# Moving the scaling multiply of two quantised feed-forward stages from VectorE to GpSimd, with the units five ahead

## The reference, cut to what matters

```
def fp4_quant_dequant(x):                 # blocks of 16 along the last dim
    scale = max(max(abs(xb)) / 6.0, 1e-12)
    xn = xb / scale
    idx = searchsorted(_MID, abs(xn))     # grid 0, .5, 1, 1.5, 2, 3, 4, 6
    return _GRID[idx] * sign(xn) * scale

gate = fp4_linear(x, w_gate)              # 128 -> 352
y    = fp4_linear(x, w_up)                # 128 -> 352
h    = silu(gate) * y
return fp4_linear(h, w_down)              # 352 -> 128

x = x + 0.5 * _L1_ffn_ref(_layernorm(x), ...)     # stages four and six
```

## Time and profile before

| | us |
|---|---|
| median of 3 runs (2184.43 to 2184.46) | 2184.46 |
| the profiled execution, its own time | 2185.35 |
| its span in the profile | 2183.3 |
| PE busy (share of the span) | 1894.8 (87%) |
| DVE busy | 1719.8 (79%) |
| ACT busy | 1094.0 (50%) |
| POOL busy | 737.7 (34%) |

### The profile page before, as it was taken

The page is one execution under the profiler, slowest core; times in us unless marked ns, Lnnn a source line. Parts: engine busy times, 40 slices in busy tenths (PEclk is TensorE's granted clock), DMA queues, the critical chain, the costliest instruction groups (busy, mean ns, idle before and its releaser), DMA issues.

```text
span 2183.3 us, 66263 instructions
## 1 busy us (share of the span) xinstructions
PE 1894.8 (87%) x27657; PEld 1452.5 (67%) x27657; DVE 1719.8 (79%) x3976; ACT 1094.0 (50%) x2876; POOL 737.7 (34%) x835
## 2 busy tenths in 40 slices
PE   0999899998999677768999999999999999767775
PEld 0888566665888455546777777777777777645553
DVE  5566688888566799976888888888888888579995
ACT  0444333332444445445666666666666666344542
POOL 1000577775000122213444444444444444212221
PEclk9999999999999799988999999999999999879997
DMA  4000000000000000000000000000000000000002
GB/s 110 1 1 2 1 2 2 2 2 1 1 1 1 1 0 1 1 1 2 3 3 3 3 3 3 3 3 3 3 3 3 3 3 3 3 1 1 1 1 77
DMA packets 14551, 14.42 MB, mean 7 GB/s; under 512 B 1392, under 2 KB 12080, under 8 KB 14256
## 3 DMA queue, kind: packets, MB, share of 16 engines
q1 hardware_dynamic: 14256, 10.20, 1.7%
HBM read 6.01 MB, written 4.19 MB: 5 GB/s over the span
## 4 chain that ended last, share of the span: by engine, by line
PE 64%; DVE 22%; POOL 5%; ACT 4%; issue 4%; SPq 0%; DVEq 0%; POOLq 0%; DMA 0%
PE acc L472 6%; PE acc L449 5%; PE acc L1652 5%; PE acc L1642 4%; POOL arena L933 4%; PE acc L749 4%; PE acc L1664 3%; DVE arena L897 3%; DVE arena L890 3%; PE acc L767 3%; DVE arena L900 3%; ACT arena L946 3%; PE acc L1694 2%; PE acc L463 2%; DVE arena L1209 2%
## 5 line engine op out<-in xcount | busy, mean ns | idle before, releaser
L1492 POOL TENSOR_TENSOR arena<-arena 128x288 f32<-128x288 f32 (+1 forms) x384 | 292.1, 767 | 460.3 <-ACT arena L1399 400.9
L933 POOL TENSOR_TENSOR arena<-arena 128x960 f32<-128x960 f32 (+2 forms) x70 | 118.0, 1685 | 576.1 <-DVE arena L900 576.1
L1399 ACT ACTIVATE arena<-acc 64x288 f32<-64x288 f32 x384 | 155.4, 405 | 143.9 <-PE acc L1670 136.4
L1218 DVE SCALAR_TENSOR_TENSOR arena<-acc,arena 128x288 f32<-128x288 f32 (+1 forms) x384 | 157.0, 409 | 71.0 <-PE acc L1664 39.9
L424 ACT ACTIVATE arena<-acc,wib 128x256 f32<-128x256 f32 x256 | 100.3, 475 | 151.2 <-PE acc L463 151.2
L1002 PE MATMUL acc<-wguT,arena 128*128 128x352 f32 x256 | 117.4, 544 | 60.5 <-DVE arena L872 57.0
L1024 PE MATMUL acc<-wdT,arena 128*128 128x128 f32 (+1 forms) x768 | 105.8, 289 | 69.9 <-ACT arena L961 69.0
L667 POOL TENSOR_TENSOR arena<-arena,quadcol 128x512 f32<-128x512 f32 x64 | 65.2, 1040 | 289.6 <-DVE arena L545 289.6
L1024 PEld LDWEIGHTS acc<-wdT,arena 128*128 128x128 f32 (+1 forms) x768 | 93.3, 196 | 85.5 <-ACT arena L961 85.5
L1664 PE MATMUL acc<-arena 64*64 64x72 f32 (+1 forms) x3072 | 135.3, 224 | 11.7 <-DVE arena L1218 11.7
L1652 PE MATMUL acc<-arena 64*64 64x72 f32 (+1 forms) x3072 | 134.0, 224 | 13.0 <-DVE arena L1209 12.6
(11 more groups left out here) (240 smaller groups left out, 4951.5 us busy)
## 6 DMA issues: line engine op xcount, KB each, us to landing
out_dram<-X SPq DMA_DIRECT2D x4, 1024.0 KB, 9.3
wi<-in_wiT_dram SPq DMA_DIRECT2D x1, 256.0 KB, 2.7
wout<-in_woT_dram SPq DMA_DIRECT2D x1, 256.0 KB, 3.3
wqkv<-in_w_qkv_dram SPq DMA_DIRECT2D x1, 192.0 KB, 2.7
arena<-in_w_down_dram SPq DMA_DIRECT2D x1, 176.0 KB, 2.5
arena<-in_w_gate_dram SPq DMA_DIRECT2D x1, 128.0 KB, 2.1
arena<-in_w_up_dram SPq DMA_DIRECT2D x1, 128.0 KB, 2.2
wq<-in_WqT_dram SPq DMA_DIRECT2D x1, 64.0 KB, 2.3
```

What stands on the lines that cost most here:

```text
L933: pool.tensor_tensor(b3(zq[s][:, cols]), b3(rnd[s][:, cols]), each(small[s][:, 1, blocks(n)]), ALU.mult).then_inc(zq_ready, 1)
L1218: dve.scalar_tensor_tensor(pm[s][:, group[g], cols], pn[s][:, group[g], cols], part, tm[s][:, group[g], cols], ALU.mult, ALU.add).then_inc ...
L1399: ins = act.mul(sq[s][rows, group[g], :], pn[s][other, group[g], 0:MW], part)
L1492: pool.tensor_tensor(tm[s][:, group[g], cols], pm[s][:, group[g], cols], sq[s][:, group[g], cols], ALU.subtract).then_inc(tm_ready, 1)
```

## The change

LEAD becomes 5, and the buffers z, y, big, rnd and zq become three deep (DEEP = 3, indexed by unit modulo 3). The pairs of small per-block arrays (scale and reciprocal) exist four times (`kept`), and two more arrays, the block maximum and the maximum with the margin (`top`), lie in PSUM bank 7 (`peak`). The turned x moves to the second half of bank 6, beside the output of `down`. The large multiply of `scale` is done by POOL (`scaled`), with the margin put into `top` by one more small instruction on DVE; y has now its true sign, so the first rounding instruction subtracts. All four programs get a new order, with scale and split of one unit three turns apart. In the last stage `finish` takes no statistics.

```
-            LEAD = 3
+            LEAD, DEEP = 5, 3
+            kept = LEAD - 1
+            last = phase == len(plan)
-            xT = psum[:, 7, 0:SEQ]
+            xT = psum[:, 6, SEQ:2 * SEQ]
+            peak = psum[:, 7, 0:2 * kept * NZ].rearrange("p (u c b) -> p u c b", u=kept, c=2)
...
                 def finish(n):
-                    for j in range(TPB):
+                    if not last:
                         dve.wait_ge(added, n + 1)
-                        dve.wait_ge(masks, 1)
-                        dve.bn_stats(...)
+                        for j in range(TPB):
+                            dve.bn_stats(...)
...
+                def scale(u):
+                    if u >= LEAD:
+                        dve.wait_ge(hid_ready, u - LEAD + 1)
+                    if u < NB:
+                        dve.wait_ge(xn_ready, u + 1)
+                    amax, top = (peak[:, u % kept, c, blocks(u)] for c in range(2))
+                    scl, inv = (small[u % kept][:, c, blocks(u)] for c in range(2))
+                    dve.tensor_reduce(amax, b3(z[u % DEEP][:, part(u)]), AX, ALU.max, apply_absolute_value=True)\
+                       .then_inc(amax_ready, 1)
+                    dve.wait_ge(amax_ready, u + 1)
+                    c = chain.did(dve.tensor_scalar(top, amax, (1.0 + 2.0 ** -22) / 6.0, 1e-12, ALU.mult, ALU.max))
+                    dve.tensor_scalar(scl, amax, 1.0 / 6.0, 1e-12, ALU.mult, ALU.max).then_inc(scl_ready, 1)
+                    chain.settle(c)
+                    dve.reciprocal(inv, top).then_inc(inv_ready, 1)
...
-                for n in range(NB):          # hidden, scale(n+3), finish(n-2), split(n+3)
+                for n in range(-LEAD, NB + 5):
+                    if 0 <= n + 2 < NB + LEAD:
+                        split(n + 2)
+                    if 0 <= n < NB:
+                        hidden(n)
+                    if 0 <= n - 5:
+                        finish(n - 5)
+                    if n < NB:
+                        scale(n + LEAD)

             def g(pool):
+                def scaled(u):
+                    k = u % DEEP
+                    pool.wait_ge(inv_ready, u + 1)
+                    pool.tensor_tensor(b3(y[k][:, part(u)]), b3(z[k][:, part(u)]), each(small[u % kept][:, 1, blocks(u)]),
+                                       ALU.mult).then_inc(y_ready, 1)
+                def restore(u):              # waits hT_done, xT_done, rnd_ready(u), scl_ready(u)
+                    ...
+                for n in range(-4, NB + 3):
+                    if 0 <= n + 2:
+                        restore(n + 2)
+                    if 0 <= n + 4 < NB + LEAD:
+                        scaled(n + 4)
...
+            ACT, n from -6: gated(n+1) twice, turned_x(n+2), magnitude(n+4), turned(n-3), norm(n+6);
+                norm(n) waits y_ready(n-3)
+            PE, n from -2: gates(n+1), turn_x(n+2), turn_hidden(n-3), down(n-4);
+                turn_x(n) waits xqT_ready(n-1) and added(n-6); turn_hidden(n) waits hqT_ready(n-1);
+                down(n) waits xqT_ready(n+6) and added(n-1)
```

More of the change, by code:

```diff
@@ L818, in fp4_ffn @@
             HX, HH = TPB * D, TPB * FH
-            LEAD = 3
+            LEAD, DEEP = 5, 3
+            U = range(DEEP)
+            kept = LEAD - 1
+            last = phase == len(plan)
             HZ = HX + HH
             NZ, NX = HZ // BLK, HX // BLK
[L823 to L827, removed]
+            z = [cut(HZ) for _ in U]
+            y = [cut(HZ) for _ in U]
+            big = [cut(HZ) for _ in U]
+            rnd = [cut(HZ) for _ in U]
+            zq = [cut(HZ) for _ in U]
             xqT = [cut(SEQ) for _ in R]
@@ L870, in hidden @@
+                def hidden(n):
                     dve.wait_ge(sig_ready, (n + 1) * TPB)
                     dve.wait_ge(up_done, (n + 1) * TPB)
[L872 to L898, removed]
-                    chain.settle(k)
-                    dve.scalar_tensor_tensor(rnd[s][:, cols], big[s][:, cols], FLOOR, rnd[s][:, cols],
+                    dve.tensor_tensor(hid[(n + LEAD) % DEEP], sig[n % STREAMS], ups, ALU.mult).then_inc(hid_ready, 1)
@@ L901, in split @@
+                def split(u):
+                    dve.wait_ge(big_ready, u + 1)
+                    k, cols = u % DEEP, part(u)
+                    c = chain.did(dve.scalar_tensor_tensor(rnd[k][:, cols], big[k][:, cols], FLOOR, y[k][:, cols],
+                                                           ALU.max, ALU.subtract))
+                    chain.settle(c)
+                    dve.scalar_tensor_tensor(rnd[k][:, cols], big[k][:, cols], FLOOR, rnd[k][:, cols],
                                              ALU.max, ALU.subtract).then_inc(rnd_ready, 1)
@@ L906, in v @@
                 dve.sem_inc(normed, 1)
-                scale(0, 0)
-                scale(1, 1)
-                split(0, 0)
-                scale(2, 0)
-                split(1, 1)
-                split(2, 0)
-                for n in range(NB):
-                    s = n % STREAMS
-                    hidden(n, s)
-                    scale(n + LEAD, 1 - s)
-                    if n >= STREAMS:
-                        finish(n - STREAMS)
-                    split(n + LEAD, 1 - s)
-                for s in R:
-                    finish(NB - STREAMS + s)
@@ L958, in turned @@
+                def turned(n):
+                    s = n % STREAMS
                     for j in range(TPB):
@@ L1029, in t @@
                 pe.wait_ge(*prepare.done)
[L1030 to L1044 removed]
+                for n in range(-2, NB + 4):
+                    if 0 <= n + 1 < NB:
+                        gates(n + 1)
+                    if n + 2 < NB:
+                        turn_x(n + 2)
+                    if 0 <= n - 3 < NB:
+                        turn_hidden(n - 3)
+                    if 0 <= n - 4 < NB:
+                        down(n - 4)
             vec.append(v), ten.append(t), sca.append(a), gps.append(g)
```

132 lines of the change are left out of this document (57 added, 75 removed).

## The result

The changed kernel takes 2109.94 us (median of 4 runs, 2103.83 to 2112.18) against 2184.46 (2184.43 to 2187.32) for the kernel before, measured beside it: a ratio of 0.9658, 95% interval 0.9645 to 0.967. The forecast was 2128 with a range from 2111 to 2154. The direction and the main mechanism were right. The gain was larger than any case allowed: 74.5 us against 56.4, and against 72.8 in the most hopeful one.

What follows compares the result with a forecast made beforehand. VectorE was taken to bound the kernel before in the two changed stages, at 7.39 us a turn. First stage -25.7 and last -30.7, together -56.4, took 2185.35 to 2129.0; the median, 0.9 lower, gave 2128, range 2111 to 2154.

Steps and rivals of the forecast that it cites:

- the most hopeful one: Whole kernel: the ends cost nothing more and the clock never drops; 72.8 us saved, 2112 us, chance 0.05.
- the port excludes, and it sets the turn: Quantised stages: VectorE's two roundings and GpSimd's multiplies exclude each other, a chain of 6.11 us, binding in the last stage.
- rival 1: GpSimd's multiplies are dearer beside VectorE, 0.25 us more each, a turn of 6.65 in both stages; 2150 us, chance 0.12.
- The wait for the magnitude: VectorE's hole before the first rounding, ended by ScalarE's magnitude, goes: -0.21 us a turn.
- +0.19: VectorE's turn: cost in us of one more small tensor_scalar, between 0.1 and 0.5.
- 6.30: First stage: VectorE's turn in us, from 7.39 - 1.07 - 0.21 + 0.19, longer than the chain with 0.1 to spare.
- 6.17: Last stage: turn in us set by the chain of two roundings and GpSimd's two multiplies, with a hand-over.
- the statistics left out in the last one: Last stage: VectorE's work falls by 0.49 us a turn, of which only 0.13 is had.
- +2.4 a stage: Both stages: three drops of TensorE's clock make `finish` late, +2.4 us a stage, between 0 and 5.
- the ends: Each stage: small units -4.5 us, filling +3.5, emptying +2.3; in the last, statistics of the last five pairs -1.5.
- Rival 3: GpSimd's scaling slips between the two roundings and holds VectorE 1.82 us more a turn; 2216 us, chance 0.06.
- A read costs nothing: VectorE reading PSUM: reciprocals of 128 columns take 948 ns from PSUM and 943 from SBUF.

Runs made afterwards that it cites:

- Experiments 2 to 4: Changed kernel with statistics in neither quantised stage, 2103.75 us; with statistics in both, 2106.64; with GpSimd leaving 256 x columns of full units unscaled, 2089.95.
- experiment 4: Changed kernel with GpSimd's scaling leaving out the 256 x columns of full units: 2089.95 us.
- experiment 3: Changed kernel with the last stage taking its statistics again, so both quantised stages take them: 2106.64 us.
- experiment 5: Changed kernel with the multiply by the reciprocal back on VectorE, all else kept: 2158.24 us.
- experiment 7: Changed kernel with TensorE doing `down` ahead of `turn_hidden` once the pairs run out: 2104.38 us.
- experiment 12: The changed kernel once more without any edit, on the same chip as the combined version: 2104.53 us.
- experiment 6: Changed kernel with the block maximum and the margined maximum in SBUF instead of PSUM: 2139.35 us.
- experiment 8: Changed kernel with VectorE scaling 128 of the 960 columns of all full units in the last stage: 2108.92 us.

## Why the prediction was right or wrong

**Right: the port excludes, and it sets the turn.** The two roundings and GpSimd's multiplies form one chain, read from one row of 256 columns. Experiments 2 to 4 show it. GpSimd's multiplies cost 1.82 each and start 1.78 apart, as taken; rival 1 is out. The wait for the magnitude is gone. The maximum is no dearer into PSUM (1.14 against 1.15). L889 and L890 take 0.14 and 0.13 by starts, where +0.19 was taken for the new one.

**Wrong: "6.30", VectorE's own turn in the first stage.** It is 5.75. The sum was made by taking instructions out of the list of starts and closing the gaps with the spacing each had before. But the spacing belongs to a pair of neighbours. In these rows, where the next instruction does not need the one in front, it starts before that one ends; where it does, after. By starts, before and in a turn of experiment 4 where nothing is held: `hidden` to its follower 0.91, now 0.80; statistics to their follower 0.49, now 0.40; first to second rounding 1.19, now 1.13; reciprocal to the next large one 0.56, now 0.45; the small ones 0.19 + 0.23, now 0.14 + 0.13. These sum to 0.52 of the 0.55. (The two roundings depend on each other in both kernels. Their 0.06 comes from the first one, itself 1.09 long behind the reciprocal and 1.16 before; no run shows why.) The kernel before held the clue: there too 0.88 of L872 was followed after 0.91 by a maximum that needed it, while 1.16 of L900 was followed after 1.08 by L872, which did not. Since the chain is longer than 5.75, the first stage went to the chain: 27 x (6.30 - 6.04) = 7.0 us more than forecast.

**Mis-sized: "6.17", the chain.** Its parts by starts: 0.23 from the end of L902 to GpSimd (taken 0.16), 1.78 to the scaling, 2.84 from there to the end of the first rounding, 0.04, and 1.16 for the second: 6.05. Without the first part, the forecast's sum came to 3.60 + 2.35 + 0.06 = 6.01 where 1.78 + 2.84 + 0.04 + 1.16 = 5.82 was measured. An undisturbed rounding is 1.09 to 1.16, so the held one starts 1.68 to 1.75 after GpSimd's scaling did, a little before the recorded end of it. 27 x 0.13 = 3.5 us in the last stage. And because the chain binds in both stages, the statistics left out in the last one brought nothing to the turn (experiment 3), where 0.13 was forecast.

**Wrong: "+2.4 a stage" for the clock.** It was 0 in the steady turns: 1.00 in both windows above, with TensorE idle 1.1 in each turn. 4.8 us in all. The step took the drops of the kernel before over into a kernel in which they don't come. Its other half, that less cover makes a drop visible, fits experiment 5: turns of 7.00 don't show the lower level, turns of 6.48 grow to between 7.2 and 7.5. It shows in the filling of the changed kernel too: at a granted clock of 0.95 over the filling the fifth turn of the first stage takes 6.75, at 1.00 that of the last stage 5.95 (in experiment 7, at 0.95, that of the last stage takes 6.75 too).

**Mis-sized: the ends.** Small units, filling and emptying were to cost +1.3 and -0.2 us. Counting from the start of the normalisation, they came to -0.8 and -2.8 (stage lengths less 36.3 and 39.1, first `hidden` 1.0 and 0.2 sooner, less the 36.5 of 27 turns of 7.39 - 6.04). That is 4.7 us. The first `hidden` was to be 0.8 later and was 1.0 earlier. Of this the clock made the most, by luck: the stretch from the start of the normalisation to it took 16.11 us before, at a granted clock of 0.58, and 15.10 after, at 0.66; but 16.17 in experiment 12, the changed kernel at 0.58. At the same clock it is neither sooner nor the 0.8 later. Rival 3's mechanism, GpSimd between the roundings, does occur, but only in the emptying, where nothing repeats it.

**The sum.** 7.0 + 3.5 + 4.8 + 4.7 = 20.0 us more than forecast in the two stages. The rest of the program was 2.8 us longer in this execution, hence 73.8 in the spans. The range was missed by 1.1 us, and not by an unlucky measurement: the same kernel's two later medians lie 4 and 6 us below the range. It missed because its low end let the clock and the ends vanish, but no shorter turn of VectorE: the one term taken as read, not estimated, had no bound of its own.

**Not seen at all: what PSUM was for.** "A read costs nothing" was true and beside the point. That a small instruction with an SBUF source stands behind GpSimd (experiment 6) would have been a rival of 2139. The prediction took the placement over and asked only what it might cost.

## What to carry to other kernels

Before moving work to GpSimd, list which VectorE instructions can run beside it: here those with two SBUF inputs cannot, nor a small `tensor_scalar` from SBUF, while a maximum, and the instructions seen here with an input in PSUM, can. The turn is then the longest of each engine's own sum and of the chain of all that excludes each other. When instructions are taken out of a list of starts, price each new pair of neighbours by a pair of the same kind, dependent or independent, and give the result a bound. A stretched instruction without a wait in front of it is a wait: compare its length with the same form elsewhere.

## What the runs showed of the hardware

- A `tensor_scalar` of 60 columns from SBUF to SBUF waits until GpSimd's two-input multiply ends (1.15 and 1.66 us), and takes 0.21 to 0.23 from PSUM beside it.
- A rounding held by GpSimd's multiply effectively starts 0.07 to 0.14 us before the recorded end of that multiply: an estimate from the 2.84 above, less 1.09 to 1.16 for the rounding, against 1.82.
- TensorE's granted clock is not a simple matter of how tight the turn is: 1.00 in steady turns of 5.82 and 6.04 us, 0.91 in turns of 7.00 and 0.89 in turns of 6.5 to 7.5 (experiment 5; the 0.91 between 840 and 900 us), 0.50 for a whole turn in one filling (experiment 8). The cause stays open. The same changed kernel had emptyings of 18.8 and 19.7 us in its last stage, so a difference of under 1 us between two stage lengths is not read as an effect either.
- The same changed kernel had medians of 2109.94, 2106.81 and 2104.53 the three times that it was measured, with stage lengths within 0.8 us of each other. The one stage between the two, 939.3 us in the kernel before and 940.5 in the changed one, lasted between 932.8 and 943.1 in the profiled runs of the others, though its code is the same in all. A gain of less than about 5 us is better read from the stage than from the median.
